# A graph layer's gather passes: PE signals by drains, other group sizes, a deeper sort ring and new last stages

## The reference

```python
def _hconv(x, W, b, src, dst, n):           # twice, PReLU behind each
    xt = x @ W
    m = segment_sum(xt[src], dst) * Binv    # mean over the edges of a dst
    return segment_sum(m[dst], src) * Dinv + b
h = _prelu(_hconv(xn, W1, b1), a)
gnn = _prelu(_hconv(h, W2, b2) + xn, a)
# mix: q, k, v of 8 heads of 64; k and v normalised; dots = k^T v; q dots / n; Wout
x = x + gnn + mix(xn)
# ffn: on the normalised x, normalised again, * gamma + beta; a router takes 2 of
# 8 experts; each is gelu(xn W1 + b1) W2 + b2, weighted by a softmax of the two
x = x + ffn(_layernorm(x))
```

## Time and profile before

| what | value |
|---|---|
| median of 3 runs | 8475.15 us (8469.13 to 8481.79) |
| profiled execution | 8563.98 us, span 8562.2 us |
| PE busy | 4688.6 us (55%) |
| DVE busy | 3784.0 us (44%) |
| POOL busy | 4105.5 us (48%) |
| ACT busy | 1385.0 us (16%) |
| POOL's gathers (line 525) | 3520, 953 ns each, idle 3058.3 us ahead of them |

### The profile page before, as it was taken

One profiled execution on the slowest core, in us unless ns is written; L12 is line 12 of the kernel. 1 busy time (PEld: TensorE's weight loads), 2 busy tenths in 40 slices (PEclk: granted clock), 3 DMA queues, 4 the chain that ended last, 5 costly groups with the idle time before them and its releaser, 6 DMA issues. The chain is left out here.

```text
span 8562.2 us, 93336 instructions
## 1 busy us (share of the span) xinstructions
PE 4688.6 (55%) x16858; PEld 2911.1 (34%) x16859; DVE 3784.0 (44%) x11251; ACT 1385.0 (16%) x4213; POOL 4105.5 (48%) x4256
## 2 busy tenths in 40 slices
PE   3116976666666645555554455445444544454796
PEld 1014533333333323333332233333223322334564
DVE  5105754444444444444444444444433433367323
ACT  0004843333333300000000000000000000000242
POOL 4761034444444445555555465566565556532342
PEclk7558988888788767787776677777666666666898
DMA  2002011222222142222223333333532222231114
GB/s 85 0 21 72 0 43 58 59 59 59 59 59 59 57 103 78 77 81 80 79 76 76 102 107 108 108 108 110 121 121 83 82 82 83 83 74 51 33 62 130
DMA packets 330997, 639.22 MB, mean 75 GB/s; under 512 B 81808, under 2 KB 201444, under 8 KB 330448
## 3 DMA queue, kind: packets, MB, share of 16 engines
q0 software_dynamic: 191808, 490.67, 21.1%
q1 hardware_dynamic: 131396, 140.16, 5.0%
q10 hardware_dynamic: 7756, 7.97, 0.3%
HBM read 551.49 MB, written 87.01 MB: 75 GB/s over the span
## 5 line engine op out<-in xcount | busy, mean ns | idle before, releaser
L525 POOL DMA_INDIRECT gbuf<-table,idxb x3520 | 3354.6, 953 | 3058.3 <-ACT idxb L650 1351.3
L1342 PE MATMUL PS<-gbuf,ohg 128*128 128x257 f32 x7040 | 2549.8, 494 | 2923.0 <-DVE acc L940 1543.0
L1342 PEld LDWEIGHTS PS<-gbuf,ohg 128*128 128x128 f32 x7040 | 1572.3, 242 | 3818.4 <-DVE acc L940 2000.4
L940 DVE TENSOR_TENSOR acc<-acc,PS 128x257 f32 x3520 | 1498.0, 426 | 2999.0 <-remote 1290.7
L949 DVE TENSOR_SCALAR ohg<-iota,dl 128x128 f32<-128x128 f16 x2664 | 796.0, 305 | 519.9 <-issue 499.9
L1311 PE MATMUL PS<-region 128*128 128x440 f16 x3328 | 851.6, 383 | 0.0
L650 ACT COPY idxb<-idx 128x4 int32 (+1 forms) x884 | 168.0, 190 | 3690.7 <-DVE acc L940 2775.5
L640 ACT ACTIVATE region<-region,acc 128x128 f16<-128x128 f16 x838 | 336.4, 401 | 1300.4 <-DVE region L891 1139.6
L1311 PEld LDWEIGHTS PS<-region 128*128 128x128 f16 x3328 | 355.3, 107 | 337.7 <-issue 100.5
L534 POOL DMA_INDIRECT scattered_d<-acc x384 | 370.2, 964 | 142.7 <-issue 120.2
L890 DVE TENSOR_SCALAR region<-iota_c,acc 128x880 f16<-128x880 f16 x838 | 394.4, 471 | 53.1 <-issue 53.1
(11 more groups left out here) (282 smaller groups left out, 3791.9 us busy)
## 6 DMA issues: line engine op xcount, KB each, us to landing
gbuf<-table,idxb POOLq DMA_INDIRECT x3520
table<-acc SPq DMA_DIRECT2D x21, 896.0 KB, 6.7
region<-xt_d SPq DMA_DIRECT2D x98, 128.0 KB
gbuf<-ye_d SPq DMA_DIRECT2D x12, 1024.0 KB, 7.8
xpad_d<-acc SPq DMA_DIRECT2D x1, 6272.0 KB, 21.8
xn_d<-acc SPq DMA_DIRECT2D x49, 128.0 KB
xt_d<-acc SPq DMA_DIRECT2D x49, 128.0 KB
table<-acc SPq DMA_DIRECT2D x49, 128.0 KB
```

The source lines that it names most:

```text
L525: gp.indirect_dma_start(gbuf[:, k, 0:F], None, tables[p], bass.IndirectOffsetOnAxis(idxb[:, k:k + 1], 0)).then_inc(s_g[k], 16)
L940: TT(a, a, PS[:, 4 + k % AB, 0:FC], ALU.add).then_inc(s_acc[p], 1)
L1342: m = MM(PS[:, 4 + k % AB, 0:FC], ohg[:, k, :], gbuf[:, k, :], start=True, stop=True)
```

## The change

1. PE signals by `signal(...)`, a drain that carries the increment, in place of the last matmul's `then_inc`: in the histograms (every second block), the ranks, the sort of order 0 (every fourth column) and all product passes.
2. Passes 0 and 1 keep groups of 2 chunks and 4 banks; passes 2 and 3 take 256 columns, half a bank a chunk, so 8 of them, and groups of 4. In pass 0 the two sort columns of a group stand behind its drain.
3. Order 1: ranks and LN products are ordered anew, one drain tells of a block's ranks and its transposes, the LN product comes behind it; SP's fence each seven blocks is replaced by three semaphores (blocks 3, 2 and 2 of seven).
4. The sort ring has 16 columns, with 8 ahead (LEAD) for 6, and moves to another buffer.
5. Between passes 1 and 2: per block one fused multiply and add, two ReLUs on ACT, one fused sum for seven blocks.
6. In eight turns of pass 3 gamma and beta are folded into the experts' weights and biases (PE, ACT and DVE), and into the router's.
7. Last stage: no scaling ahead of the transpose (the inverse is applied behind the product), one norm in place of two, with eps worked in, ACT normalises, nothing on POOL, skip and residual double-buffered, PE's order written out.

```diff
-    AB = 4
-    GP = 2
-    RING = 8
+    RING = 16
+    def width(p):
+        return FC if p < 2 else F
+    def banked(p):
+        return 4 if p < 2 else 8
+    def group(p):
+        return 2 if p < 2 else 4
     SG = 4
-    LEAD = 6
+    LEAD = 8
...
-    sp.wait_ge(s_lnd, (i + 1) * (48 * R7))
-    sp.sem_inc(s_lnfree, 1)
...
+            def normalized(b):
+                if b >= R7 and b % R7 in (0, 3, 5):
+                    n = PART_OF[b % R7]
+                    act.wait_ge(s_lnd[n], b // R7 * PART[n] * 48)
...
             def add_chunk(p, i, k, block_of):
-                if k % GP == 0:
-                    dve.wait_ge(s_mm[p], i * (U // GP) + (k // GP + 1))
+                if k % group(p) == 0:
+                    dve.wait_ge(s_mm[p], i * (U // group(p)) + (k // group(p) + 1))
                 dve.wait_ge(s_acc[p], i * U + (U + k))
...
-                TT(a, a, PS[:, 4 + k % AB, 0:FC], ALU.add).then_inc(s_acc[p], 1)
+                TT(a, a, chunk_sum(p, k), ALU.add).then_inc(s_acc[p], 1)
...
+                for b in range(n * R7, (n + 1) * R7):
+                    m = STT(out=accs[1][:, b, 0:F], in0=accs[1][:, b, 0:F], scalar=inv[:, 1, b:b + 1], in1=vecs[:, 0, :],
+                            op0=ALU.mult, op1=ALU.add)
...
+            def fold_beta(i, k):
+                if k == 8:
+                    dve.wait_ge(s_fold, i - FOLD + 2)
+                    b = fa_["b1r"][:, ds(i - FOLD, 1), :].rearrange("p a h -> p (a h)")
+                    TT(b, b, PS[:, 0, :], ALU.add).then_inc(s_shift, 1)
...
-                    m.then_inc(s_hist, 1)
+                    if b % 2 or b == NB - 1:
+                        signal(s_hist)
...
             for b in range(NB):
                 rank(0, b)
+                signal(s_rank)
...
+            for b in range(NB + 2):
+                if b < NB:
+                    pe.wait_ge(s_xn, b + 1)
+                    for kt in range(KT):
+                        TR(PS[:, 4 + b % 2, kt * P:(kt + 1) * P], ln["xn"][:, b % R7, kt * P:(kt + 1) * P], ident[:, :])
+                    rank(1, b)
+                signal(s_rank)
+                if 1 <= b <= NB:
+                    pe.wait_ge(s_xtc, b)
+                    for kt in range(KT):
+                        MM(PS[:, 6 + (b - 1) % 2, 0:F], ln["xt"][:, (b - 1) % R7, kt * P:(kt + 1) * P],
+                           ln["w1"][:, kt, :], start=kt == 0, stop=kt == KT - 1)
...
                 if o == 0 and k % SG == SG - 1:
-                    m.then_inc(s_used, 1)
+                    signal(s_used)
...
-                        if k % GP == 0:
-                            pe.wait_ge(s_acc[p], i * U + (U + k + GP - AB))
-                        m = MM(PS[:, 4 + k % AB, 0:FC], ohg[:, k, :], gbuf[:, k, :], start=True, stop=True)
-                        if k % GP == GP - 1:
-                            m.then_inc(s_mm[p], 1)
+                        if k % group(p) == 0:
+                            pe.wait_ge(s_acc[p], i * U + (U + k + group(p) - banked(p)))
+                        MM(chunk_sum(p, k), ohg[:, k, :], gbuf[:, k, 0:width(p)], start=True, stop=True)
                         if body is not None:
                             body(i, k)
+                        if k % group(p) == group(p) - 1:
+                            signal(s_mm[p])
+                            if columns:
+                                for c in range(k + 1 - group(p), k + 1):
+                                    sort_column(1, i, c)
```

More of the change, by code:

```diff
@@ L548, in _ @@
                 pool.wait_ge(s_sc[h], SC_TURNS * U * 16)
-            pool.wait_ge(s_lnfree, NR7 + 1)
+            for n in range(3):
+                pool.wait_ge(s_lnd[n], NR7 * PART[n] * 48)
             pool.wait_ge(s_wd, 32)
@@ L565, in _ @@
             gather_pass(3)
[L568 to L577, removed]
             pool.wait_ge(s_ei, 1)
@@ L622, in _ @@
             act.wait_ge(s_ln, 1)
[L623 to L635, removed]
+            def normalized(b):
+                if b >= R7 and b % R7 in (0, 3, 5):
+                    n = PART_OF[b % R7]
+                    act.wait_ge(s_lnd[n], b // R7 * PART[n] * 48)
+                A(ln["xn"][:, b % R7, :], x_sb[:, b, :], ACT.Identity,
+                  bias=mean_c[:, b:b + 1], scale=rstd_c[:, b:b + 1]).then_inc(s_xn, 1)
+            normalized(0)
+            for b in range(NB + 2):
+                if b + 1 < NB:
+                    normalized(b + 1)
+                act.wait_ge(s_rank, NB + b + 1)
+                if b >= 2:
+                    A(ln["t1"][:, (b - 2) % R7, :], PS[:, 6 + b % 2, 0:F], ACT.Copy).then_inc(s_t1c, 1)
+                if b < NB:
+                    A(ln["xt"][:, b % R7, :], PS[:, 4 + b % 2, 0:F], ACT.Copy).then_inc(s_xtc, 1)
             def sort_column(o, i, k):
@@ L1327, in _, with product_pass @@
             close_sort(0)
-            def product_pass(p, start, end, body=None):
+            def product_pass(p, start, end, body=None, columns=False):
                 if start == 0:
@@ L1413, in _, with fold_body @@
             product_pass(2, NB, TURNS)
-            product_pass(3, 0, TURNS)
+            def fold_body(i, k):
+                if k == 4:
+                    pe.wait_ge(s_shift, i - FOLD + 3)
+                    for kt in range(KT):
+                        m = MM(PS[:, 0, :], fa_["shift"][:, kt, :], fr["w1"][:, ds(i - FOLD, 1), kt, :].rearrange("p a h -> p (a h)"),
+                               start=kt == 0, stop=kt == KT - 1)
+                    signal(s_fold)
+            product_pass(3, 0, FOLD)
+            pe.wait_ge(s_shift, 1)
+            for kt in range(KT):
+                m = MM(PS[:, 1, 0:NE], fa_["shift"][:, kt, :], fr["wr"][:, kt, :], start=kt == 0, stop=kt == KT - 1)
+            signal(s_fold)
+            product_pass(3, FOLD, FOLD + NE, fold_body)
+            product_pass(3, FOLD + NE, TURNS)
             pe.wait_ge(s_fw, N_FW)
             pe.sem_inc(s_lgc, 1)
+            pe.wait_ge(s_fin, 3 * NR7 + 1)
             def transposed(bank, source, n):
@@ L1448, in pe_third @@
                 m.then_inc(s_lg, 1)
-            by_group(pe, pe_first, pe_second, pe_third)
+            for q in range(2):
+                turn_sums(q, G)
+                second_weights(q, q, G)
+            for q in range(1, NG - 1):
+                turn_sums(q + 1, G)
+                turn_rows(q - 1, (q - 1) % 2, G)
+                second_weights(q + 1, (q + 1) % 2, G)
+                logits(q - 1, G)
+            turn_sums(NG, 1)
+            turn_rows(NG - 2, 0, G)
+            second_weights(NG, 0, 1)
+            logits(NG - 2, G)
+            turn_rows(NG - 1, 1, G)
+            logits(NG - 1, G)
+            turn_rows(NG, 0, 1)
+            logits(NG, 1)
             pe.wait_ge(s_ecnt, 1)
```

247 lines of the change are left out of this document (138 added, 109 removed).

## The result

The changed kernel takes 8724.58 us (8715.69 to 8731.68, four runs), the kernel before 8478.47 (8469 to 8497, four runs): a ratio of 1.0287, 95% interval 1.0267 to 1.0307. Forecast were 8702 us and slower with a chance of 0.57. The profiled execution took 8724.92, its span 8722.8, so 161 us more than before's 8563.98; the medians differ by 246. The kernel before varies more from run to run (8469 to 8564 with the profiled one) than the changed one (16 us in all), and its profiled execution is the longest of its five.

A forecast was written before the change was run, and what follows sets the result against it. In the passes no engine was busy throughout; late signals, PE's pace and DVE's queue held back POOL's gathers. Terms summed to +229 on the profiled 8563.98, so 8793, times 0.9896 gave 8702 us, range 8280 to 8880.

The forecast's parts named there:

- A free drain costs 0.5 us of PE: On PE where no signal is late: a drain adds about 0.32 + 0.17 = 0.5 us.
- Sort of order 0, +56: Order 0 sort, PE without gaps: 112 drains at 0.5 us add 56 us, from 0 to +60.
- Pass 0, +156: Pass 0: of eight drains a turn two hide, six cost 3 us, x52 = +156 us, from 0 to +208.
- Pass 1, +72: Pass 1: eight drains a turn, a third of 4 us shows, 1.3 x55 = +72 us, from 0 to +220.
- Passes 2 and 3, +35: Passes 2 and 3: four half-hidden drains, partly repaid by fewer DVE waits, +0.3 us a turn, x110; bounds -275 to +330.
- fold, +25: Pass 3: folding beta and gamma lengthens eight turns by 2.5 us, split loop 5: +25 us, from 0 to +40.
- Between passes 1 and 2, -25: Between passes 1 and 2: a seven-block piece falls from 9.17 to 5 us; -25 us, from -30 to -15.
- Last stage, -105: Last stage: DVE falls to about 8 us a group, PE sets the pace; -105 us, from -80 to -130.
- Histogram and ranks, +15 and 0: Order 0 drains before the scatters +15 us (0 to +37); order 1, mostly beside the scatters, 0 (-20 to +25).
- hidden drains: Rival for the passes: drains hide behind late signals and DVE, leaving the certain gains, some 8330 us; chance 0.24.
- prompt drains: Rival for the passes: matmul signals come late, drains don't, halving DVE's pass 0 waits; near 7900 us; chance 0.12.
- Much slower: Rival for the passes: late drains close PE, 2 us more in each of 220 turns, +440, 9135 us; chance 0.12.

The follow-up runs named there:

- experiment 1: Changed kernel with each product group's signal carried by its last matmul again in all four passes, other drains kept: 8481.98 us, ratio 0.9926 to the kernel before.
- 2: Changed kernel with the product groups' signals on matmuls again in pass 0 alone: 8546.83 us, ratio 1.0008 to the kernel before.
- experiment 3: Changed kernel with the signal of each fourth column of the order 0 sort on a matmul: 8682.16 us, ratio 1.0175 to the kernel before.
- experiment 4: Kernel before, changed only so that each group of two products signals by a drain in all four passes: 8794.37 us, ratio 1.0312.
- experiment 5: Changed kernel with groups of 2 chunks on four banks in passes 2 and 3 too, drains kept: 8755.95 us, ratio 1.0324 to the kernel before.
- experiment 6: Changed kernel with ACT's copy of the turned router rows ahead of the next group's norm in the last stage: 8648.61 us, ratio 1.0193 to the kernel before.
- 7: Changed kernel with products' and sort's signals on matmuls and ACT's router copy ahead of the next norm: 8357.39 us, ratio 0.9848 to the kernel before.
- 8: Changed kernel with products', sort's, histograms' and ranks' signals on matmuls and ACT's router copy ahead of the next norm: 8346.84 us, ratio 0.9841 to the kernel before.

## Why the prediction was right

The direction and the main cause were right, the time too, in part by errors that cancelled; some terms weren't.

- **A free drain costs 0.5 us of PE.** The sort gives 0.48, a free stretch of pass 0 0.39 (2.74 - 2.35). That drains are what made the kernel slower is shown by experiments 1 to 4.
- **Sort of order 0, +56:** +54, undone by experiment 3.
- **Pass 0, +156:** +139. The size was right, and what it is made up of isn't settled. With the change's other edits in place, pass 0 takes 2073 to 2082 us in the four kernels with drains in it (the changed one, 3, 5 and 6) and 1899 to 1905 in the four without (1, 2, 7 and 8), by the gathers of each, so drains cost some 180. Put into the kernel before, they cost 133 (experiment 4). So with drains the other edits win nothing, as the text had it ("doesn't shorten PE's work"), and without them they seem to win 42. But that rests on the only trace of the kernel before on such a chip, an execution 89 us above its median. Either the edits and the drains don't simply add, or that pass 0 was long by chance. 133 to 180 us are 0.32 to 0.43 for each of 416 drains, at a price of 0.39, so the six of eight in the text are neither confirmed nor refuted.
- **Pass 1, +72:** +16 by the profiled executions, 79 by experiment 1, 26 by experiment 4. Pass 1 took 1475 to 1538 us in four kernels with matmul signals and 1554 to 1567 in those with drains, so the sign is sure and the size, some 20 to 80, isn't.
- **Passes 2 and 3, +35, and fold, +25:** +5 together. Experiment 5 shows that groups of four with half the drains win 31 us over groups of two, and experiment 1 that pass 3 is 46 shorter and pass 2 18 longer without them. A cost of the fold can't be seen apart from this; the turns with it weren't run by themselves.
- **Between passes 1 and 2, -25:** -23. A piece takes 4909.63 - 4904.86 = 4.77 us, as these rows show (answer to the earlier trace rows); 5 was forecast.

```profile
4904.86 2.08 DVE L1074 SCALAR_TENSOR_TENSOR acc<-region,small,acc 128x1792 f32<-128x1792 f32 x1 [0.58 <-ACT acc L703]
4906.86 2.85 DVE L1078 SCALAR_TENSOR_TENSOR acc<-acc,inv,vecs 128x256 f32<-128x256 f32 x7
4909.63 2.08 DVE L1074 SCALAR_TENSOR_TENSOR acc<-region,small,acc 128x1792 f32<-128x1792 f32 x1
```

- **Last stage, -105:** -38 from the last gather to the first matmul behind the stage (7579.0 to 7866.6 before, 7775.4 to 8024.6 after). This is the step that was most off. DVE's work fell as forecast, from 18 us a group to 8.8, but the group didn't go to PE's pace of 11; it stayed at 18.3 by an order of ACT's queue. I priced each engine's work and didn't follow the new copies and norms through ACT's queue in order. With the order changed the stage is 187.0 us, from 7773.2 to 7960.2, and so 101 shorter than before (experiment 6): the forecast's number, for another kernel. The first matmuls behind the stage, in the kernel before, the changed one and experiment 6:

```profile
L1454 PE MATMUL PS<-ohg,lower x2: 362/370/379, 7866.6 to 7866.9; 128*128 128x8 f32 x2
L1542 PE MATMUL PS<-ohg,lower x2: 362/370/379, 8024.6 to 8024.9; 128*128 128x8 f32 x2
L1548 PE MATMUL PS<-ohg,lower x2: 361/370/379, 7960.2 to 7960.4; 128*128 128x8 f32 x2
```

- **Histogram and ranks, +15 and 0:** +7 and about -6; the sort starts at 783 in both.
- **The rivals:** hidden drains and prompt drains are refuted by experiments 1 and 4. "Much slower" had the right picture, PE closed for 10.6 us behind a drain, but it took no 2 us a turn more: DVE's two long waits sum to 15.9 us, and were 16.0. The 11.84 us of the earlier trace rows are weak evidence for it by themselves, as their row names DVE's one-hot (line 949) and not the drain as what ended the wait; the 10.62 us of the changed kernel have no such other cause in their row.
- **Slips in the working:** "over 2000 drains" is a miscount, the trace has 1695. "Near 7900" for much faster doesn't follow from its terms: 2 us a turn less in three passes is 330, and with the rest that gives some 7700. The bounds of the parts add up to far more than 8560 to 8850, a span which the text doesn't derive.

That 8702 lies so near to 8724.58 is in part luck. The sum was made for the profiled execution and gave 8793, 68 us more than the 8724.92 measured: +229 for +161. Passes 1 to 3 with the fold were 110 too dear, pass 0 17, what stands ahead of it 15, and the last stage 67 too cheap. The factor 0.9896 then took off 91, on the ground that a profiled execution is longer than a median one. For the changed kernel it wasn't (8724.92 and 8724.58). The two errors nearly cancelled.

## What to carry to other kernels

In this kernel a drain as a signal cost PE about 0.4 to 0.5 us each, wherever PE set the pace, and was as late as a matmul's signal where signals were late; put it where the engine waits anyway, or leave the increment on the matmul. When an engine's work is moved to another in a software-pipelined loop, read the receiving engine's queue in order and ask which instruction of the group behind it is now waited for; halving the busiest engine's work bought 38 us, and moving one copy 62 more. Weigh a change on more than one chip before it is kept.

## What was not expected of the hardware

- The same kernel before took 8478 us beside the changed kernel and in the second set, 8538 in the first, and 6363 on the third chip: a quarter less. The difference is in stretches where POOL issues indirect DMAs: a pass 0 of 1190 us for 1943, and the order-1 work beside the scatters. The scatters themselves, the sort of order 0 (335 us) and what follows the last gather take the same within 1 to 2%. The lateness of the earlier trace rows thus goes with the chip, or with its state at the time, and not with the program; why wasn't found.
- Runs of kernels whose products signal by matmuls reach over 0.3 to 1.2% on the late chips, those with drains in all passes over 0.2 to 0.7%, and all over 0.1 to 0.2% on the prompt one.
- With the drain in front of the eight records of the columns, DVE's long waits changed from 7.21 + 8.77 to 10.64 + 5.24, nearly the same sum (a third of 2.27 follows it): what comes late seems to be set by the burst of gathers, not by how the signal is carried. That was only read, not tried.
